# Node stages of a graph-network kernel: loads and stores of one 512-row group each become loads and stores of a 1024-row pair

## The chip, the cores and the metric

The kernel runs on one core of one Trainium2 chip. The metric is device time in microseconds (us) of one execution. All data are float32 and the tables live in HBM.

## The reference, cut to what matters

A table `x` of 50000 nodes by 128 features passes through four residual graph layers over the same 25000 edges (`src`, `dst`, sorted by `dst`):

```
h = relu(layernorm(x)); x = x + relu(segment_sum(h[src] @ W[edge_type], dst) + h @ W_loop + b)   # REL
h = relu(layernorm(x)); x = x + attention(q(h[dst]), k,v(h[src]), softmax over the edges of dst) # ATT
h = relu(layernorm(x)); x = x + sage(relu(layernorm(sage(h))))                                   # SAGE0, SAGE1
h = relu(layernorm(x)); x = x + degree-normalised sum over neighbours and self of h @ W          # GCN
```

## The kernel before, in words

There are five phases: REL, ATT, SAGE0, SAGE1 and GCN. Each has an **edge stage** and then a **node stage**. The edge stage goes through the edges in 49 rounds (`ROUNDS`) of 4 tiles of 128: GpSimd (POOL) gathers source rows, the engines compute messages and sum them over equal destinations, and the sums are scattered to a table in HBM (`sums` or `attsums`). In SAGE0, SAGE1 and GCN the segment sums of all rounds stay in SBUF (`parked`) and are scattered only when the edge stage is over, while the node stage already runs (`scatter_parked`, L854, four indirect DMAs a round). The node stage follows ("chases") these rounds.

The node stage goes through the nodes in 98 groups (`GROUPS`) of 512 rows. A group lies in SBUF as 4 rows a partition (`K = 4`) over 128 partitions; a row of a table between phases has 132 numbers (`W`, 528 B), a row of the input `x` and of `out` has 128. For each group SyncE (SP) loads the rows (`load_x`, L672) and the sums (`load_s`, L699), in SAGE1 also the residual rows (`load_x2`, L708), and stores the result (`store`, L722). The data of one partition in one such DMA are contiguous on both sides, 2112 B (2048 B for `x` and `out`). There are 8 slots each for inputs and results in `ring`, and 8 for sums in `edge_cells`. ScalarE (ACT) normalises, TensorE (PE) turns and multiplies, VectorE (DVE) computes moments, adds and scales; the results of a group are ready 4 to 7 groups after its rows were first touched.

Each engine runs its own list of steps, written by `run_steps`: a list of (step, lag) and a loop over groups; in turn g a step with lag n handles group g - n. Steps wait on semaphores, and an engine takes its instructions strictly in order. For SP the list is `load_x` at lag 0, `load_s` at lag 0, 2 or 3, `load_x2` at lag 5, `store` at lag 6 to 10. A wait in `load_x` is for the slot to be free (`n_turned`, `n_y_used`, `x_added` or `row_ready` of group g - 8). The wait in `load_s` is for the slot and, in the four phases with segment sums, for the scattered rounds that the group needs: their number stands in a small table `due_i` and is read into an SP register for every group (`value_load`, L691 and L697 in the profile, shown as TENSOR_LOAD), and then SP waits for `rounds_landed` (or `kept_landed` in REL). `store` waits for `row_ready` of its group. `out_free` makes the engine that writes a result slot, and `load_x2` on SP, wait until the store 8 groups earlier has landed (`stored`).

In the edge stage of ATT, SP also loads every second group of `rows1` into SBUF ahead of the node stage (`keep_x`), so that the node stage of ATT loads only the other half.

Of the kernel before, what the change touches and what calls it, by code (L numbers as in the profile page):

```python
# [103 lines left out]
def gnn_stack_kernel(nc, x, src, dst, edge_type, w_rel, w_loop, b_loop, w_q, w_k, w_v,  # L104
# [8 lines left out]
    P = 128  # L113
# [27 lines left out]
    LAST_ROWS = N - (GROUPS - 1) * GROUP  # L141
    assert LAST_ROWS % K == 0

# [23 lines left out]
    with ctx:  # L167
# [241 lines left out]
        loaded = [Signal(sem(f"loaded{s}"), 16) for s in range(SLOTS)]  # L409
        loaded_s = [Signal(sem(f"loaded_s{s}"), 16) for s in range(SLOTS)]  # L410
        loaded2 = [Signal(sem(f"loaded2_{s}"), 16) for s in range(SLOTS)]
        stored = [Signal(sem(f"stored{s}"), 16) for s in range(SLOTS)]
# [77 lines left out]

        def loads_before(phase, s):

            return stores_before(phase, s) - (stores_before(1, s) if phase > ATT and s % 2 == 0 else 0)

        def stores_before(phase, s):

            return phase * (GROUPS // SLOTS + (1 if s < GROUPS % SLOTS else 0))
# [16 lines left out]
        def dense(slot):  # L514

            return ring_cells[:, slot * K * W:slot * K * W + K * D].rearrange("p (k d) -> p k d", k=K)

        def kept(phase, g):

            return phase == ATT and g.mod(2) == 0  # L520

        def kept_rows(g):

            return spans[:, bass.ds(g.div(2).scaled(K * W), K * W)].rearrange("p (k c) -> p k c", k=K)

        def x_data(phase, g):

            if kept(phase, g):
                return kept_rows(g)[:, :, 0:D]
            return dense(g.mod(8)) if phase == REL else x_rows(phase, g)[:, :, 0:D]  # L530

        def x_cols(phase, g, c):

            if phase == REL:
                at = g.mod(8) * K * W + K * D + (c - COL_A) * K
                return ring_cells[:, at:at + K]
            return x_rows(phase, g)[:, :, c]

        def x_col(phase, g, k, c):

            if phase == REL:
                at = g.mod(8) * K * W + K * D + (c - COL_A) * K + k
# [3 lines left out]
        def out_data(phase, g):  # L546

            return dense(SLOTS + g.mod(SLOTS)) if phase == GCN else out_rows(phase, g)[:, :, 0:D]

        def x_landed(eng, phase, g):  # L550
            s = g.mod(SLOTS)
            if kept(phase, g):
                eng.wait_ge(s_kept, 16 * ROUNDS)
                return
            eng.wait_ge(loaded[s].sem, loaded[s].after(g.div(SLOTS), loads_before(phase, s)))

        def s_landed(eng, phase, g):
            s = g.mod(SLOTS)
            eng.wait_ge(loaded_s[s].sem, loaded_s[s].after(g.div(SLOTS), stores_before(phase, s)))
# [35 lines left out]
        def _(sp):  # L595
# [24 lines left out]
            for phase in range(5):  # L620

                def keep_x(r):
                    sp.wait_ge(a_h.sem, a_h.after(r))
                    rows = rows1[bass.ds(r.scaled(2 * GROUP), GROUP), :]
                    sp.dma_start(kept_rows(Step(r.i, 2 * r.times, 2 * r.offset)), rows.rearrange("(p k) c -> p k c", k=K))\
                        .then_inc(s_kept, 16)

                if phase == ATT:
                    for s in range(SLOTS):
# [10 lines left out]
                if phase > 0:  # L640
                    for s in range(SLOTS):
                        sp.wait_ge(stored[s].sem, 16 * stores_before(phase, s))

                def span(g):
                    if g.i is None and g.offset == GROUPS - 1:
                        return slice(N - GROUP, N)
                    return bass.ds(g.scaled(GROUP), GROUP)

                def at(g):
                    return bass.ds(g.scaled(1), 1)  # L650
# [1355 lines left out]
```

## Time and profile before

| | |
|---|---|
| Median of 3 runs | 3517.78 us (3517.47 to 3519.11) |
| The profiled execution, its own time | 3518.85 us |
| Its span, first to last instruction | 3517.1 us |
| Instructions | 66658 |
| Moved by DMA | 638.06 MB, 328005 packets |

A span is counted from the first instruction. The five node stages lie at about 527 to 840, 1525 to 1780, 2052 to 2338, 2606 to 2954 and 3225 to 3514 us; the edge stages are between them. Busy times of an engine are sums of its instructions; the DMA share is the mean busy share of the 16 DMA engines; PEclk is the granted TensorE clock as a share of full speed.

### The profile page before, as it was taken

Reading aid. Unit: us, or ns where it says so; the run is one execution under the profiler, and the core shown is the slowest. Engines: PE = TensorE matmul, PEld = TensorE weight load, DVE = VectorE, ACT = ScalarE, POOL = GpSimd, SP = SyncE. Lnnn points to the kernel's source line nnn. Section 1 sums busy time; section 2 is a strip of 40 time slices with the busy share of each in tenths; the row PEclk is TensorE's granted clock in tenths of the full one; section 3 lists DMA queues with packets and bytes.
Section 4 is the critical chain, followed back from the end, with each engine's and each line's share of the span. In section 5 each row is a group of like instructions: output and inputs, shape, how many; then the busy total and the mean of one; then the engine's idle time right before and its main releaser. Section 6 shows DMA issues by size and latency. Waiting matters only on the chain. (4 is left out here: it accounts for less than half of the span.)

```text
span 3517.1 us, 66658 instructions
## 1 busy us (share of the span) xinstructions
PE 2430.4 (69%) x14044; PEld 1912.0 (54%) x14044; DVE 2493.7 (71%) x10828; ACT 1710.1 (49%) x4561; POOL 2471.2 (70%) x2428
## 2 busy tenths in 40 slices
PE   5988878995666665600058887756678885666998
PEld 3444437774555555500058775545567664555777
DVE  6887869995645545469966678864448887556998
ACT  2333327885544444401134467841126664556777
POOL 5777757777888888745567777847778772777774
PEclk9999999998877777755555679975579997557999
DMA  7355539995444444358832269962249996223998
GB/s 268 127 213 218 212 127 292 315 311 168 69 60 62 62 60 62 55 174 268 268 98 52 52 220 317 314 203 53 52 133 353 340 345 198 53 52 110 319 316 287
DMA packets 328005, 638.06 MB, mean 181 GB/s; under 512 B 61062, under 2 KB 89766, under 8 KB 321762
## 3 DMA queue, kind: packets, MB, share of 16 engines
q1 hardware_dynamic: 233176, 501.53, 42.5%
q0 software_dynamic: 90944, 133.85, 17.3%
q10 hardware_dynamic: 3786, 1.65, 0.2%
q14 instruction: 72, 0.59, 0.1%
q8 instruction: 27, 0.44, 0.1%
HBM read 371.35 MB, written 277.04 MB: 184 GB/s over the span
## 5 line engine op out<-in xcount | busy, mean ns | idle before, releaser
L798 POOL DMA_INDIRECT got<-rows,gidx x588 | 602.3, 1024 | 251.7 <-issue 169.9
L854 POOL DMA_INDIRECT sums<-parked,tidx x588 | 603.8, 1027 | 172.2 <-issue 160.8
L1132 ACT ACTIVATE n_h<-ring 128x128 f32<-128x128 f32 x1176 | 484.0, 482 | 153.7 <-issue 115.0
L1411 PE MATMUL bank<-edge_cells,ident 128*128 128x128 f32 x2352 | 460.8, 278 | 0.0
L1268 PE MATMUL bank<-ident,edge_cells 128*128 128x128 f32 x588 | 137.8, 379 | 386.9 <-ACT edge_cells L999 386.2
L1278 PE MATMUL bank<-parked 128*128 128x512 f32 x784 | 367.0, 611 | 52.9 <-DVE parked L1670 46.7
L868 POOL DMA_INDIRECT attsums<-ring,sidx x196 | 312.5, 1595 | 80.6 <-issue 62.8
L1411 PEld LDWEIGHTS bank<-edge_cells,ident 128*128 128x128 f32 x2352 | 363.0, 195 | 0.0
L1562 DVE COPY gidx<-src_i 128x4 int32 (+1 forms) x225 | 43.5, 193 | 409.1 <-DMA got<-rows,gidx 201.9
L1268 PEld LDWEIGHTS bank<-ident,edge_cells 128*128 128x128 f32 x588 | 94.7, 191 | 433.4 <-ACT edge_cells L999 359.5
L1408 PE MATMUL bank<-w_t,n_ht 128*128 128x128 f32 x1568 | 289.0, 299 | 57.3 <-DMA edge_cells<-sums 56.8
L999 ACT ACTIVATE edge_cells<-got 128x128 f32<-128x128 f32 x588 | 242.0, 483 | 137.3 <-DMA got<-rows,gidx 90.0
L1408 PEld LDWEIGHTS bank<-w_t,n_ht 128*128 128x128 f32 x1568 | 225.7, 201 | 109.9 <-DMA edge_cells<-sums 80.6
L1640 DVE TENSOR_TENSOR_SCAN edge_cells<-bank,edge_cells 128x512 f32<-128x512 f32 x196 | 249.8, 1275 | 43.4 <-ACT edge_cells L1024 15.0
L798 POOL DMA_INDIRECT got<-rowsg,gidx x196 | 195.3, 996 | 93.1 <-issue 51.2
L1278 PEld LDWEIGHTS bank<-parked 128*128 128x128 f32 x784 | 144.0, 194 | 212.2 <-issue 166.7
L1348 PE MATMUL bank<-ident,edge_cells 128*128 128x128 f32 x392 | 82.6, 348 | 249.3 <-ACT edge_cells L1072 249.2
L798 POOL DMA_INDIRECT got<-in_x_dram,gidx x196 | 198.0, 1010 | 72.9 <-issue 54.2
L916 POOL DMA_INDIRECT parked<-rows,dst_i x196 | 195.3, 997 | 74.1 <-issue 65.4
L1670 DVE SCALAR_TENSOR_TENSOR parked<-bank,edge_cells 128x512 f32<-128x512 f32 x392 | 242.0, 682 | 5.2 <-issue 5.2
L1384 PE MATMUL bank<-ident,n_h 128*128 128x128 f32 x1176 | 194.7, 290 | 72.5 <-ACT n_h L1132 55.8
L817 POOL DMA_INDIRECT sums<-edge_cells,sidx x148 | 146.1, 987 | 99.3 <-ACT edge_cells L1038 55.0
(191 smaller groups left out, 6444.8 us busy)
## 6 DMA issues: line engine op xcount, KB each, us to landing
edge_cells<-sums SPq DMA_DIRECT2D x392, 264.0 KB
ring<-rows SPq DMA_DIRECT2D x343, 264.0 KB, 4.3
rows<-ring SPq DMA_DIRECT2D x291, 264.0 KB
edge_cells<-attsums SPq DMA_DIRECT2D x98, 264.0 KB
ring<-rowsg SPq DMA_DIRECT2D x98, 264.0 KB
rowsg<-ring SPq DMA_DIRECT2D x97, 264.0 KB
sums<-parked SPq DMA_DIRECT2D x16, 1584.0 KB
attsums<-parked SPq DMA_DIRECT2D x16, 1584.0 KB
```

The costliest lines, as they stand in the source:

```text
L798: pool.indirect_dma_start(out=got[:, b, j, 0:width], out_offset=None, in_=table[:, :], in_offset=bass.IndirectOffsetOnAxis(ap=gidx[:, b, j ...
L854: pool.indirect_dma_start(out=sums[:, :], out_offset=bass.IndirectOffsetOnAxis(ap=tidx[:, r % 4, j:j + 1], axis=0), in_=parked[:, t, :], i ...
L868: pool.indirect_dma_start(out=attsums[:, :], out_offset=bass.IndirectOffsetOnAxis(ap=sidx[:, b, j:j + 1], axis=0), in_=att_out[:, b, j, :] ...
L916: pool.indirect_dma_start(out=parked[:, t, :], out_offset=None, in_=rows1[:, :], in_offset=bass.IndirectOffsetOnAxis(ap=dst_i[:, t:t + 1], ...
L999: last = nc.scalar.activation(e_h[:, b, j, :], got[:, c, j, 0:D], ACT.Relu, bias=got[:, c, j, COL_C:COL_C + 1], scale=got[:, c, j, COL_A:C ...
L1132: last = nc.scalar.activation(n_h[:, b, k, :], x_data(phase, g)[:, k, :], ACT.Relu, bias=x_col(phase, g, k, COL_C), scale=x_col(phase, g, ...
L1268: last = nc.tensor.transpose(bank[0][:, j * P:(j + 1) * P], rows, ident[:, :])
L1278: last = nc.tensor.matmul(bank[1][:, :], lhsT=w_rel_sb[:, rel, :], rhs=e_htm[:, b, rel, :], start=(rel == 0), stop=(rel == NREL - 1))
L1408: last = nc.tensor.matmul(o, lhsT=n_ht[:, b, k * P:(k + 1) * P], rhs=node_w[phase], start=(bias is None), stop=(not summed and k == K - 1))
L1411: last = nc.tensor.matmul(o, lhsT=ident[:, :], rhs=s_rows(phase, g)[:, k, 0:D], start=False, stop=(bias is None or k == K - 1))
L1640: nc.vector.tensor_tensor_scan(run_t[:, b, :], flag_bank[b][:, :], msg_t[:, b, :] if phase == REL else e_ht[:, b, :], 0.0 if fresh else ru ...
L1670: last = nc.vector.scalar_tensor_tensor(out=e_htm[:, b, rel, :], in0=type_bank[b][:, :], scalar=float(rel), in1=e_ht[:, b, :], op0=ALU.is_ ...
```

## The change

Two neighbouring groups form a pair of 1024 rows (`PAIR`, 49 `PAIRS`): a partition now holds 8 consecutive rows of a table, 4224 B (4096 B for `x` and `out`), of which the first group of the pair takes four and the second the other four. SP's node loop runs over pairs, with 4 pair slots (`PAIR_SLOTS`) in the same memory as the 8 group slots. All other engines still work by groups. A wait that asked for group g now asks for the second group of the pair (`second_of`), and `due_i` and the counts for `fetch_dst` are by pairs. SP's list of steps is `load_x`, `store`, `load_x2`, `load_s`, with new lags. `keep_x` keeps every second pair. The last pair has 848 rows and is stored by two DMAs (96 and 10 partitions).

```diff
+    PAIRS = GROUPS // 2
+    PAIR = 2 * GROUP
+    PAIR_SLOTS = 4
...
+        def pair_of(g):
+            return g.div(2)
+        def second_of(h):
+            return Step(h.i, h.times * 2, h.offset * 2 + 1)
...
+        def pair_cells(tensor, first_slot, h, size):
+            at = (first_slot + 2 * h.mod(PAIR_SLOTS)) * K * W
+            return tensor[:, at:at + size]
+        def by_rows(cells):
+            return cells.rearrange("p (k c) -> p k c", k=2 * K)
...
-        def out_free(eng, phase, g):
-            if g.i is None and g.offset < SLOTS:
+        def out_free(eng, phase, h):
+            if h.i is None and h.offset < PAIR_SLOTS:
                 return
-            o = g.back(SLOTS)
-            s = o.mod(SLOTS)
-            eng.wait_ge(stored[s].sem, stored[s].after(o.div(SLOTS), stores_before(phase, s)))
+            o = h.back(PAIR_SLOTS)
+            s = o.mod(PAIR_SLOTS)
+            eng.wait_ge(stored[s].sem, stored[s].after(o.div(PAIR_SLOTS), stores_before(phase, s)))
...
                 def keep_x(r):
+                    if r.mod(2) == 0:
+                        return
+                    h = r.back(1)
                     sp.wait_ge(a_h.sem, a_h.after(r))
-                    rows = rows1[bass.ds(r.scaled(2 * GROUP), GROUP), :]
+                    rows = rows1[bass.ds(h.scaled(PAIR), PAIR), :]
...
-                def load_x(g):
-                    s = g.mod(SLOTS)
+                def load_x(h):
+                    s = h.mod(PAIR_SLOTS)
+                    g = second_of(h)
...
-                    table = node_in[phase]
-                    sp.dma_start(x_data(phase, g) if phase == REL else x_rows(phase, g), table[span(g), :].rearrange("(p k) c -> p k c", k=K))\
+                    rows = by_rows(pair_cells(ring_cells, 0, h, 2 * K * (D if phase == REL else W)))
+                    sp.dma_start(rows, node_in[phase][span(h), :].rearrange("(p k) c -> p k c", k=2 * K))\
                         .then_inc(loaded[s].sem, 16)
...
-                        due = sp.value_load(due_i[0:1, CHASED.index(phase), at(g)], min_val=base, max_val=base + ROUNDS)
+                        due = sp.value_load(due_i[0:1, CHASED.index(phase), at(h)], min_val=base, max_val=base + ROUNDS)
                         sp.wait_ge(rounds_landed.sem, due)
...
-                s_lag = {REL: 2, ATT: 0, SAGE0: 2, SAGE1: 3, GCN: 2}[phase]
-                store_lag = {REL: 9, ATT: 6, SAGE0: 9, SAGE1: 10, GCN: 7}[phase]
-                stages = [(load_x, 0), (load_s, s_lag), (load_x2, 5), (store, store_lag)]
+                store_lag = {REL: 5, ATT: 4, SAGE0: 6, SAGE1: 6, GCN: 4}[phase]
+                stages = [(load_x, 0), (store, store_lag), (load_x2, 3), (load_s, 0 if phase == ATT else 1)]
                 if phase == REL:
-                    stages.append((row_stored, store_lag + 2))
-                run_steps(sp, stages, GROUPS, SLOTS, behind=SLOTS)
+                    stages.append((row_stored, store_lag + 1))
+                run_steps(sp, stages, PAIRS, PAIR_SLOTS, behind=PAIR_SLOTS)
```

The order of SP's instructions in the loop of SAGE0's node stage, before, for one group (ISA and REGISTER_ALU rows are waits and register arithmetic; `edge_cells` holds the sums, `ring` the rows, `rowsg` is the result table):

```order
L672 ISA [waits n_turned]
L672 DMA ring<-rows 128x528
L682 REGISTER_ALU
L697 ISA [waits n_y_used]
L697 TENSOR_LOAD due_i
L697 ISA x2
L699 ISA [waits rounds_landed]
L699 DMA edge_cells<-sums 128x528
L714 REGISTER_ALU
L722 ISA [waits row_ready]
L722 DMA rowsg<-ring 128x528
```

The same place in the changed kernel, for one pair:

```order
L727 ISA [waits n_turned]
L727 DMA ring<-rows 128x1056
L771 REGISTER_ALU
L781 ISA [waits row_ready]
L781 DMA rowsg<-ring 128x1056
L738 REGISTER_ALU
L753 ISA [waits n_y_used]
L753 TENSOR_LOAD due_i
L753 ISA x2
L755 ISA [waits rounds_landed]
L755 DMA edge_cells<-sums 128x1056
```

The number of instructions of a turn is the same, but a turn now serves two groups. The store has moved ahead of the load of the sums, which now stands behind the store's wait.

SP's loop in SAGE1's node stage before, for one group (`stored3` is the semaphore of a store slot, L708 the load of the residual rows):

```order
L697 ISA [waits mid_sd_ready]
L697 TENSOR_LOAD due_i
L697 ISA x2
L699 ISA [waits rounds_landed]
L699 DMA edge_cells<-sums 128x528
L567 ISA
L708 ISA [waits stored3]
L708 DMA ring<-rows 128x528
L714 REGISTER_ALU
L722 ISA [waits row_ready]
L722 DMA rows<-ring 128x528
```

The same place in the changed kernel, for one pair (L765 loads the residual rows):

```order
L727 DMA ring<-rowsg 128x1056
L771 REGISTER_ALU
L781 ISA [waits row_ready]
L781 DMA rows<-ring 128x1056
L765 ISA [waits stored2]
L765 DMA ring<-rows 128x1056
L740 REGISTER_ALU
L753 ISA [waits mid_sd_ready]
L753 TENSOR_LOAD due_i
L753 ISA x2
L755 DMA edge_cells<-sums 128x1056 [waits rounds_landed]
```

Here the wait for an earlier store to land (`stored2`) comes one turn after that store was issued, and the load of the sums is queued behind it. Before, that store had been issued three turns of one group earlier, and the load of the sums came ahead of this wait.

## Rows read from the trace of the kernel before

**Rows 1.** The page: engines busy over the span, and the DMA share in 40 slices.

```profile
PE 2430.4 (69%) x14044; PEld 1912.0 (54%) x14044; DVE 2493.7 (71%) x10828; ACT 1710.1 (49%) x4561; POOL 2471.2 (70%) x2428
...
DMA  7355539995444444358832269962249996223998
```

**Rows 2.** Stretches inside REL, ATT, SAGE0, SAGE1 (two) and GCN; columns as headed.

```profile
core 0: us, PE busy (x) PEld busy (x) DVE busy (x) ACT busy (x) POOL busy (x), PEclk, DMA share, GB/s
...
616.00:704.00 88.00, 81.15 (x603) 67.30 (x603) 87.27 (x605) 71.70 (x201) 66.17 (x67) 1.00 0.97 315
...
1584.00:1672.00 88.00, 0.00 (x0) 0.00 (x0) 87.25 (x452) 10.11 (x34) 43.32 (x35) 0.50 0.82 269
...
2112.00:2200.00 88.00, 68.43 (x391) 48.86 (x390) 72.22 (x329) 69.31 (x181) 67.91 (x79) 0.92 0.98 317
...
2640.00:2728.00 88.00, 73.57 (x542) 61.35 (x540) 78.80 (x338) 56.52 (x181) 72.28 (x72) 0.98 1.02 354
2728.00:2816.00 88.00, 71.73 (x516) 60.49 (x514) 74.91 (x318) 53.27 (x172) 69.00 (x74) 0.96 1.00 337
...
3256.00:3344.00 88.00, 79.29 (x607) 69.02 (x606) 80.04 (x458) 70.01 (x182) 69.63 (x86) 1.00 0.97 319
```

**Rows 3.** DVE lines run once a group (L1958 four times): ns min/median/max, first to last start.

```profile
L1873 DVE SCALAR_TENSOR_TENSOR ring<-bank,ring x98: 650/660/693, 539.9 to 835.3; 128x512 f32<-128x512 f32 x98
...
L1896 DVE TENSOR_TENSOR n_t<-edge_cells,den x98: 691/695/969, 1528.1 to 1775.1; 128x512 f32<-128x512 f32 x98
...
L1907 DVE TENSOR_TENSOR n_t<-bank,edge_cells x98: 654/692/693, 2054.4 to 2331.9; 128x512 f32<-128x512 f32 x98
...
L1949 DVE TENSOR_TENSOR ring<-n_h,ring x98: 676/686/704, 2627.7 to 2953.2; 128x512 f32<-128x512 f32 x98
...
L1958 DVE SCALAR_TENSOR_TENSOR ring<-bank,ring x392: 338/343/353, 3233.7 to 3514.1; 128x128 f32<-128x128 f32 x196
```

**Rows 4.** Waits of SP from 2020 to 2340 us: us in total, times, longest.

```profile
SPq L722 <- DVE ring L1921: 9.1, 7, 2.1
SPq L699 <- POOLq L840: 8.8, 7, 3.1
```

**Rows 5.** Timeline of SP's DMA issues in SAGE0: start, duration.

```profile
2150.13 0.34 SPq L699 DMA_DIRECT2D edge_cells<-sums  x1
2150.74 0.35 SPq L722 DMA_DIRECT2D rowsg<-ring  x1
2151.28 0.34 SPq L672 DMA_DIRECT2D ring<-rows  x1
2153.36 0.33 SPq L699 DMA_DIRECT2D edge_cells<-sums  x1
```

**Rows 6.** Line 697, SP's register load in SAGE0, SAGE1 and GCN.

```profile
L697 SPq TENSOR_LOAD <-due_i x294: 262/698/1214, 2050.8 to 3501.2; - x147
```

**Rows 7.** Waits of the engines: SAGE0 (first two) and SAGE1, us, times, longest.

```profile
ACT n_h L1132 <- DMA ring<-rows: 37.5, 49, 2.1
DVE n_t L1907 <- DMA edge_cells<-sums: 26.0, 34, 3.7
...
PE bank L1408 <- DMA edge_cells<-sums: 51.8, 67, 2.0
```

**Rows 8.** Line 854, POOL's scatters beside SAGE0, SAGE1 and GCN: first to last start.

```profile
L854 POOL DMA_INDIRECT sums<-parked,tidx x196: 966/974/1499, 2042.0 to 2306.5; - x196
...
L854 POOL DMA_INDIRECT sums<-parked,tidx x196: 966/985/2026, 2599.9 to 2888.7; - x196
...
L854 POOL DMA_INDIRECT sums<-parked,tidx x196: 964/972/1025, 3219.3 to 3475.7; - x196
```

**Rows 9.** Two early stretches: tables are zeroed from rows of 12672 B a partition.

```profile
50.00:60.00 10.00, 9.75 (x37) 4.81 (x37) 8.34 (x24) 2.91 (x7) 1.45 (x2) 1.00 0.79 325
60.00:70.00 10.00, 9.75 (x37) 4.80 (x36) 8.88 (x25) 3.39 (x8) 3.95 (x4) 1.00 0.76 311
```

**Rows 10.** The page's DMA issues: the last number is the median us from issue to landing.

```profile
ring<-rows SPq DMA_DIRECT2D x343, 264.0 KB, 4.3
```

More of the change, by code:

```diff
@@ L640, in _, with span, at @@
                 if phase > 0:
-                    for s in range(SLOTS):
+                    for s in range(PAIR_SLOTS):
                         sp.wait_ge(stored[s].sem, 16 * stores_before(phase, s))
[L644 to L650, printed above, removed]
-                def load_x(g):
-                    s = g.mod(SLOTS)
-                    if kept(phase, g):
+                def span(h):
+                    if is_last(h):
+                        return slice(N - PAIR, N)
+                    return bass.ds(h.scaled(PAIR), PAIR)
+                def at(h):
+                    return bass.ds(h.scaled(1), 1)
+                def load_x(h):
+                    s = h.mod(PAIR_SLOTS)
+                    g = second_of(h)
+                    if kept(phase, h):
                         return
@@ L661, in load_x @@
                         sp.wait_ge(x_added.sem, x_added.before(g, SLOTS))
-                    elif phase == SAGE0:
-                        sp.wait_ge(n_turned.sem, n_turned.before(g, SLOTS, first(MATMUL, phase)))
-                    elif phase == SAGE1:
+                    elif phase in (SAGE0, SAGE1):
                         sp.wait_ge(n_turned.sem, n_turned.before(g, SLOTS, first(MATMUL, phase)))
@@ L700, in load_s, with load_x2 @@
                         .then_inc(loaded_s[s].sem, 16)
[L702 removed]
+                def load_x2(h):
                     if phase != SAGE1:
                         return
[L705 to L722 removed]
@@ L725, in row_stored, with store @@
-                def row_stored(g):
-                    s = g.mod(SLOTS)
-                    sp.wait_ge(stored[s].sem, stored[s].after(g.div(SLOTS), stores_before(phase, s)))
+                    s = h.mod(PAIR_SLOTS)
+                    out_free(sp, phase, h)
+                    sp.dma_start(by_rows(pair_cells(ring_cells, SLOTS, h, 2 * K * W)),
+                                 rows2[span(h), :].rearrange("(p k) c -> p k c", k=2 * K)).then_inc(loaded2[s].sem, 16)
+                def store(h):
+                    s = h.mod(PAIR_SLOTS)
+                    sp.wait_ge(row_ready.sem, row_ready.after(second_of(h), phase * GROUPS))
+                    table = node_out[phase]
+                    rows = by_rows(pair_cells(ring_cells, SLOTS, h, 2 * K * (D if phase == GCN else W)))
+                    if is_last(h):
+                        for low, high in ((P - LAST_PARTS, P - LAST_PARTS + LAST_EVEN), (P - LAST_PARTS + LAST_EVEN, P)):
+                            sp.dma_start(table[N - (P - low) * 2 * K:N - (P - high) * 2 * K, :]
+                                         .rearrange("(p k) c -> p k c", k=2 * K), rows[low:high, :, :])\
+                                .then_inc(stored[s].sem, 16)
+                        return
+                    sp.dma_start(table[span(h), :].rearrange("(p k) c -> p k c", k=2 * K), rows)\
+                        .then_inc(stored[s].sem, 16)
@@ L728, in row_stored @@
+                def row_stored(h):
+                    s = h.mod(PAIR_SLOTS)
+                    more = 1 if is_last(h) else 0
+                    sp.wait_ge(stored[s].sem, stored[s].after(h.div(PAIR_SLOTS), stores_before(phase, s) + more))
                     sp.sem_inc(rows_stored.sem, 1)
-                s_lag = {REL: 2, ATT: 0, SAGE0: 2, SAGE1: 3, GCN: 2}[phase]
-                store_lag = {REL: 9, ATT: 6, SAGE0: 9, SAGE1: 10, GCN: 7}[phase]
-                stages = [(load_x, 0), (load_s, s_lag), (load_x2, 5), (store, store_lag)]
+                store_lag = {REL: 5, ATT: 4, SAGE0: 6, SAGE1: 6, GCN: 4}[phase]
@@ L777, in _ @@
                 if phase > 0:
-                    for s in range(SLOTS):
+                    for s in range(PAIR_SLOTS):
                         pool.wait_ge(stored[s].sem, 16 * stores_before(phase, s))
```

121 lines of the change are left out of this document (66 added, 55 removed).

## The prediction

> **What bounds the kernel now.** I read the page first [rows 1]. No engine is above 71% over the span, so no single one is the bound, and the DMA row swings between 2 and 9 tenths: the edge stages leave the DMA engines mostly idle, the node stages fill them. The change touches almost nothing but the node stages, so each of the five was read alone, in stretches of 88 us [rows 2], with the pace of a DVE instruction that runs once a group [rows 3]. Pace is last start minus first start over 97:
>
> - REL: 295.4 / 97 = 3.05 us a group. DVE is busy 87.27 of 88 us, so it needs 3.02 us a group. DVE is the bound.
> - ATT: 247.0 / 97 = 2.55 us. DVE is busy 87.25 of 88 us. DVE is the bound; DMA is at 0.82.
> - SAGE0: 277.5 / 97 = 2.86 us. DVE is busy 72.22 of 88, 2.35 us a group; ACT 2.25. DMA is at 0.98.
> - SAGE1: 325.5 / 97 = 3.36 us. DVE 76.9 of 88 (mean of its two rows), 2.93 us a group. DMA is at 1.01.
> - GCN: 280.4 / 97.75 (four instructions a group) = 2.87 us. DVE 80.04 of 88, 2.61 us; PE 79.29 of 88, 2.59 us. DMA is at 0.97.
>
> So REL and ATT can gain nothing from transfers, and the other three have 0.51, 0.43 and 0.26 us a group that DVE doesn't need. What takes that time? The engines do wait for loads: in SAGE0 ACT 37.5 us for rows and DVE 26.0 us for sums, in SAGE1 PE 51.8 us for sums [rows 7]. Two things can make loads late, and both show. First, the DMA engines are full [rows 2]. Second, SP, which issues the loads, has hardly any wait in 320 us round SAGE0: 9.1 and 8.8 us [rows 4]. Its slots are free and its stores are ready when it comes to them. A queue that is ahead of its consumers would wait for slots; this one never does. Its turn is three DMA issues (0.34 + 0.35 + 0.34 = 1.03 us) and, between the load of rows and the next load of sums, a gap of 1.74 us [rows 5], mostly the register load, 262 ns at best and 698 at the median [rows 6]. With the small instructions between them this fills the 2.86 us. **SP's own instruction stream is the pace of SAGE0, SAGE1 and GCN**, close beside the DMA engines; SAGE1 has one issue more and is 0.50 us slower.
>
> **The change, part by part.**
>
> *SP.* A turn has the same instructions but serves two groups: about 2.9 us for 5.7 us of work (SAGE1 3.4 for 6.7). SP stops being a bound, by a factor of two. Gain on that score: all that DVE leaves free, until something else binds.
>
> *DMA engines, price of a row.* Before there is no plain load or store of 4224 B, so it is bounded. ATT's stretch has no other traffic: 269 GB/s at share 0.82 is 20.5 GB/s an engine while busy, 103 ns for 2112 B [rows 2]. Zeroing with 12672 B rows moves 311 to 325 GB/s at 0.76 to 0.79, 25.6 GB/s an engine, 495 ns a row [rows 9]. Ends: no cheaper a byte (206 ns for 4224 B), or as cheap as 12672 B (165 ns). A line through both rows gives 103 + 2112 x 0.0371 = 181 ns; I take that, 12% off, since 4224 is nearer to 2112. Some five sixths of the traffic in these stages is SP's, the rest POOL's scatters, which don't change. DMA time a group: SAGE0 0.98 x 2.86 = 2.80 us, less 10% = 2.52; SAGE1 3.39, less 10% = 3.05; GCN 2.78, less 10% = 2.50.
>
> *The scatters that the node stages chase.* 196 indirect DMAs serve 98 groups, two a group. Their pace is 264.5 / 97.5 = 2.71 us a group in SAGE0, 2.96 in SAGE1 and 2.63 in GCN, the last almost POOL's own pace [rows 8]. A pair needs the same round as its two groups did (1024 nodes against about 1024 nodes a round), so no wait is added. But a node stage can't end before its scatters. In SAGE0 they end at 2306.5 and the last DVE row starts at 2331.9 in rows 3; in GCN at 3475.7 against 3514.1. A tail of about 12 to 15 us must stay (one pair's load, then the lags).
>
> *Sum of the stages.* The largest need rules. SAGE0: scatters 2.66 against 2.86, 0.20 x 98 = 20 us; held by the scatters' tail I take 18. SAGE1: DMA 3.05 and its unevenness, 3.12; 0.24 x 98 = 23, I take 22. GCN: scatters 2.63 to DVE 2.61 with small gaps, 2.67; 0.20 x 98 = 20, I take 18. REL: 0.03 x 98 = 3 at most, I take 0. ATT: 0.
>
> *Start and end of each stage.* The first load is twice as large and the first store waits for two groups. 270 KB at about 320 GB/s is 0.85 us, once in and once out, less where the other engines are still busy; the last pair takes two DMAs. About +1.2 us x 5 = +6.
>
> *Costed at nothing.* The loads of rows in REL and GCN are issued later against their use. In GCN `load_x` of pair h+1 waits for the row of group 2h-5 (lag 4), so it goes out when DVE is some 2.5 groups before that pair; it was 3.5. That is 6.5 us; a landing takes 4.3 us at the median [rows 10] and 0.85 more for twice the bytes. Cover stands, with 1.4 us to spare; without it each us costs 49 us a stage. The store now stands ahead of the sums and can hold them back: they still go out 3.5 groups (9 us) before use in GCN and ATT, and land after some 5 to 6. In SAGE1 `load_x2` waits for a store issued one turn (6.2 us) before, which should have landed. `keep_x`: 24 DMAs for 49, hidden in the edge stage. POOL's `fetch_dst` in REL: the same rounds behind the same nodes. Instructions of PE, ACT and DVE: unchanged.
>
> Sum: -18 - 22 - 18 + 6 = -52 us. Against the profiled execution's own 3518.85 us that is 3466.9; the median of the runs is 1.1 us lower, and I give 3466.
>
> **The rivals.**
>
> *The bytes bind, not the rows.* If 4224 B cost the DMA engines 206 ns, DMA time stays 2.80, 3.39 and 2.78 us a group, and only the share below 1 is left: 0.06 x 98 = 6 us in SAGE0, 0 in SAGE1, 9 in GCN, less 6 for the ends: about 3509. For it: the share is 0.97 and above in four node stages. Against it: the 25.6 GB/s of the long rows, and that SP doesn't wait.
>
> *A ceiling on the memory side.* SAGE1 already moves 354 GB/s in one stretch, the others 315 to 319 [rows 2]. If about 355 is the most that this core gets, whatever the rows, SAGE1 gains little: its mean is 345, so 3% at best, and 22 shrinks to 8; the other two stay at 18 (they'd move 340): 3480. For it: no stretch of any kind shows more than 354. Against it: zeroing reached its 325 with the engines only 0.79 busy. The Trainium skill ("DMA: Bandwidth & Descriptors", Specifications) puts HBM at about 358 GB/s per core, which speaks for this rival; the same page's larger figures speak against it, and this trace shows no stretch that decides.
>
> *Slower: the pair loads come too late.* The place is `load_x` in REL and GCN and the sums in SAGE1, where the lead shrank or a landing wait came in ahead. It decides when a pair needs longer than its lead of about 2.5 groups: 7.6 us in REL, 6.5 in GCN. If store, sums and rows of a turn queue behind each other, 3 x 1.7 + 3.5 = 8.6 us, so REL would lose 1.0 x 49 = 49 us and GCN, at 2.1 us a pair against a gain of 0.4, about 83. Were half of the pairs hit in both: +66, SAGE0 and SAGE1 -40, ends +6: 3551. Against it: rows are issued at the head of a turn in REL and GCN, when the earlier ones have drained.
>
> *The DMAs don't get longer rows* (a lowering that cuts them at 4 rows): SP's relief stays, the rest is as with the bytes: 3509.
>
> **How the numbers follow.** Forecast 0.54. Bytes bind 0.13 and no longer rows 0.03, both at 3509, 9 us faster, with the ends of the stages as their largest doubt: half of it within 0.2%. Memory ceiling 0.16. Late pairs 0.14. 0.2% is 7 us, about what a measurement of this kernel can tell from no change. Faster: 0.54 + 0.16 + 0.08 = 0.78; same 0.08; slower 0.14. The likeliest case alone: if all three reach their floors (DVE 2.35 with the scatters' tail, -25; 2.93, -42; 2.61, -22; ends at 0) 3430; with half of each gain and ends of +10 3500. The range for 8 in 10 takes in the ceiling and the byte case: 3434 to 3514.
>
> **What would show it.** Right: TENSOR_LOADs halve; SP waits for slots or rows in SAGE0, SAGE1 and GCN; their paces 2.66, 3.12 and 2.67; packets under 8 KB fall by some 70000 or more; REL and ATT keep 3.05 and 2.55; DMA share of SAGE0 falls below 0.98. Wrong: DMA share at 1.0 with the GB/s of before (bytes), SAGE1 stuck at 3.3 and 355 GB/s (ceiling), or DVE in REL or GCN waiting on DMA for rows (late pairs). A larger drop than 85 us would mean the edge stages or REL moved as well, which nothing here explains.

## The result, and the profile after

The changed kernel is slower: 3543.85 us median (3542.24 to 3550.32, 4 runs) against 3518.26 for the kernel before (3517.47 to 3519.11, 4 runs), ratio 1.0074 with a 95% interval of 1.0061 to 1.0086. The forecast was 3466, in a range of 3434 to 3514. The profiled execution took 3542.24 us, its span 3540.5, 23.4 us more than the span of before.

The page of the changed kernel: the rate in 40 slices of the span, and the packets.

```profile
GB/s 266 127 218 219 216 132 282 306 304 151 67 60 60 64 60 64 60 122 266 272 143 52 52 163 320 288 271 52 52 78 377 380 366 176 52 52 129 318 290 279
DMA packets 215273, 637.97 MB, mean 180 GB/s; under 512 B 48578, under 2 KB 77282, under 8 KB 209036
```

The same bytes, in 215273 packets instead of 328005: the rows are longer, as meant. The totals tell no more, so the stages are read again: first the once-a-group DVE lines (they answer to [rows 3], in the order REL, ATT, SAGE0, SAGE1, GCN), then stretches of the stages to lay beside [rows 2]; SAGE1 and GCN start later now, so SAGE1's first stretch is left out and GCN's lies 44 us further on.

```profile
L1933 DVE SCALAR_TENSOR_TENSOR ring<-bank,ring x98: 652/660/692, 538.6 to 833.9; 128x512 f32<-128x512 f32 x98
...
L1956 DVE TENSOR_TENSOR n_t<-edge_cells,den x98: 691/694/1616, 1556.7 to 1803.4; 128x512 f32<-128x512 f32 x98
...
L1967 DVE TENSOR_TENSOR n_t<-bank,edge_cells x98: 650/691/693, 2085.1 to 2364.8; 128x512 f32<-128x512 f32 x98
...
L2008 DVE TENSOR_TENSOR ring<-n_h,ring x98: 673/680/704, 2663.1 to 2962.2; 128x512 f32<-128x512 f32 x98
...
L2017 DVE SCALAR_TENSOR_TENSOR ring<-bank,ring x392: 339/343/352, 3243.5 to 3536.7; 128x128 f32<-128x128 f32 x196
```

```profile
616.00:704.00 88.00, 81.12 (x605) 67.26 (x603) 87.27 (x604) 72.02 (x202) 57.40 (x59) 1.00 0.92 303
1584.00:1672.00 88.00, 0.00 (x0) 0.00 (x0) 87.33 (x457) 10.39 (x35) 44.23 (x36) 0.50 0.75 268
2112.00:2200.00 88.00, 69.61 (x407) 49.38 (x405) 72.77 (x337) 71.66 (x186) 66.38 (x79) 0.94 0.95 319
...
2728.00:2816.00 88.00, 81.53 (x619) 68.73 (x618) 87.96 (x380) 66.70 (x206) 69.00 (x70) 1.00 1.00 382
3300.00:3388.00 88.00, 79.47 (x604) 68.48 (x602) 79.19 (x452) 69.75 (x182) 61.40 (x76) 1.00 0.96 312
```

From these rows the 23.4 us can be laid out. REL and ATT keep their length (295.3 and 246.7 us). SAGE0 is 2 us longer (279.7 for 277.5), SAGE1 26 shorter (299.1 for 325.5), GCN 13 longer (293.2 for 280.4). The largest piece is where the prediction has no term: from REL's last DVE row to ATT's first there are 722.8 us for 692.8, **30 us more**, in an edge stage that the change hardly touches. The rest, the other stretches between and around the stages together, is 5 us.

In REL's stretch above DVE is as busy as before, but POOL runs 59 instructions for 67. Its line there is the fetch of destination rows (`fetch_dst`, L916 before, L976 after), which gathers, round by round, rows that REL's node stage has just stored. Of before, and then of the changed kernel, with the first gather of ATT's edge stage:

```profile
L916 POOL DMA_INDIRECT parked<-rows,dst_i x196: 991/997/1047, 590.8 to 854.2; - x196
```

```profile
L976 POOL DMA_INDIRECT parked<-rows,dst_i x196: 992/997/1047, 591.2 to 882.4; - x196
its engine sat idle before it (us, times) until:
  issue: 96.3, 176
  DMA parked<-rows,dst_i: 5.8, 19
...
886.57 1.02 POOL L858 DMA_INDIRECT got<-rows,gidx  x1 [0.18 <-issue]
```

The same 196 indirect DMAs of 1.0 us now end 28 us later. POOL issues the first gather of ATT's edge stage right behind the last of them, at 886.57 us for 858.69 before, so that stage starts 28 us later too. The timeline of POOL at one moment of REL shows how, before and after (start, duration, idle before):

```profile
704.52 1.00 POOL L916 DMA_INDIRECT parked<-rows,dst_i  x1 [0.30 <-issue]
705.82 0.99 POOL L916 DMA_INDIRECT parked<-rows,dst_i  x1 [0.30 <-issue]
707.12 0.99 POOL L916 DMA_INDIRECT parked<-rows,dst_i  x1 [0.30 <-issue]
```

```profile
703.47 1.00 POOL L976 DMA_INDIRECT parked<-rows,dst_i  x1 [0.30 <-issue]
705.87 1.00 POOL L976 DMA_INDIRECT parked<-rows,dst_i  x1 [1.40 <-issue]
...
709.77 1.00 POOL L976 DMA_INDIRECT parked<-rows,dst_i  x1 [0.30 <-issue]
712.15 1.00 POOL L976 DMA_INDIRECT parked<-rows,dst_i  x1 [1.38 <-issue]
```

Before, a round of four takes 4 x 1.30 = 5.20 us without a gap at this moment. After, every fourth start is 1.1 us late here; over the whole fetch it is 28 us in 49 rounds, 0.6 us a round. The profile puts the gap down to "issue" and names no releaser. What stands there in the code is `dst_landed(r - 1)`: POOL issues round r, then waits until round r - 1 has landed. Before, that wait was nearly always met in time (e5 below takes it away there and gains 2 us in the fetch). The scatters in the node stages have the same form (`round_landed(r - 1)`), and they are slower too: in GCN, 283.9 us for 256.4.

```profile
L914 POOL DMA_INDIRECT sums<-parked,tidx x196: 967/974/1028, 3229.5 to 3513.4; - x196
```

So the theory for the experiments: with the transfers of pairs in place POOL's indirect DMAs land later, and POOL, which waits for each round one round later, has less slack than that. And for SAGE1: its gain comes from relieving SP, not from cheaper rows.

### The profile page after: what moved, and what is told of

Same layout as the page of the kernel before. It is cut to its first block and busy times, and to the rows that moved or that the text cites. A ratio compares the mean times of both kernels' runs of the same rounds, so it can differ in the third digit from the quotient of the medians.

```text
span 3540.5 us, 63369 instructions
## 1 busy us (share of the span) xinstructions
PE 2430.0 (69%) x14044; PEld 1918.2 (54%) x14044; DVE 2487.0 (70%) x10828; ACT 1713.6 (48%) x4561; POOL 2474.9 (70%) x2428
## 2 busy tenths in 40 slices
DMA packets 215273, 637.97 MB, mean 180 GB/s; under 512 B 48578, under 2 KB 77282, under 8 KB 209036
## 5 line engine op out<-in xcount | busy, mean ns | idle before, releaser
L1059 ACT ACTIVATE edge_cells<-got 128x128 f32<-128x128 f32 x588 | 242.0, 483 | 141.0 <-DMA got<-rows,gidx 93.8
L976 POOL DMA_INDIRECT parked<-rows,dst_i x196 | 195.6, 998 | 102.4 <-issue 96.3
L1130 ACT ACTIVATE edge_cells<-got 128x128 f32<-128x128 f32 x196 | 94.8, 484 | 262.1 <-DMA got<-rows,gidx 262.1
```

The source lines that it names most:

```text
L1059: last = nc.scalar.activation(e_h[:, b, j, :], got[:, c, j, 0:D], ACT.Relu, bias=got[:, c, j, COL_C:COL_C + 1], scale=got[:, c, j, COL_A:C ...
```

## The experiments

All times below are medians beside runs of the kernel before on the same chip, and the ratios are to those runs. The medians of the kernel before lay between 3518.3 and 3522.4 us, so a difference between two medians of different experiments is uncertain by some 4 us; the ratios are the safer comparison. Stage times are first to last start of the once-a-group DVE line, from one profile each. Two profiles with the same code in a stage differ there: the changed kernel and e1 have 293.2 and 289.3 us in GCN, with its scatters at 283.9 and 278.7, and e3 and e7 have 269.8 and 263.1 us in SAGE0. Smaller differences than these say nothing.

**e1_fetch: the fetch may run two rounds ahead.** The changed kernel, with

```diff
-        fetched = [... for b in range(2)]
+        fetched = [... for b in range(4)]
...
                         fetch_dst(r)
-                        if r > 0:
-                            dst_landed(r - 1)
+                        if r > 1:
+                            dst_landed(r - 2)
+                    dst_landed(ROUNDS - 2)
                     dst_landed(ROUNDS - 1)
```

> The changed kernel, with one thing different: in REL POOL's fetch_dst waits for a round of gathers only after two more rounds have been issued (four semaphores in place of two), where it waited after one. Theory A (POOL's round loop is paced by the landing of the round before, which the pair loads make later): the gathers' pace returns from 291.2 us for 195 steps to about 263, as before the change, the attention edge stage starts some 28 us earlier, and the time falls from 3543.9 to about 3516. Theory B (the gathers get less of the DMA engines beside rows of 4224 B, whatever POOL waits for): the pace stays near 6.0 us a round and the time within 5 us of 3543.9.

Measured: 3515.0 us, ratio 0.9983 (0.9973 to 0.9992), 29 below the changed kernel's median, 32 by the ratios. The fetch of this kernel:

```profile
L976 POOL DMA_INDIRECT parked<-rows,dst_i x196: 993/1000/1050, 597.5 to 860.2; - x196
```

262.7 us, POOL's own pace, with all pair DMAs in place. ATT's first row comes at 1534.4 instead of 1556.7, though this run's REL began 4 us later. The missing term is this wait.

**e2_scatter: the scatters may run half a round further ahead.** The changed kernel, with four semaphores for the scatters and the wait for round r - 2 in the middle of round r:

```diff
                     for j in range(TPR):
+                        if j == 2 and r > 1:
+                            round_landed(r - 2)
+                            gate(pool)
...
                     for r in range(ROUNDS):
                         scatter_parked(r)
-                        if r > 0:
-                            round_landed(r - 1)
+                    round_landed(ROUNDS - 2)
```

> The changed kernel, with one thing different: in SAGE0, SAGE1 and GCN POOL waits for a round of scatters half a round later (after two tiles of the round after next; four semaphores). Theory A: the scatters' pace beside GCN goes from 2.91 us a group back to about 2.63 and beside SAGE0 from 2.82 to about 2.65, and since these two node stages wait for the rounds, GCN becomes 15 to 25 us and SAGE0 10 to 18 us shorter: about 3510. Theory B (the scatters get less of the DMA engines): both paces and the time stay, 3540 to 3546. A third reading, that the node stages are held by their own late pair loads: the scatters speed up and the stages don't, 3540.

Measured: 3519.39 us, ratio 0.9989 (0.998 to 0.9999). The scatters take 260.6, 287.5 and 252.3 us (changed kernel 275.4, 293.8, 283.9), and the node stages 265.4, 294.0 and 282.7 (279.7, 299.1, 293.2): 14, 5 and 10.5 us less. The median is 24 us below the changed kernel's, 30 by the ratios.

**e3_both: both edits together.**

> The changed kernel with both of the edits to POOL's waits. Theory A: the gains add, 28 + 33 us: about 3483, some 35 us below the kernel before the change. Theory B: no more than 5 us below 3543.9.

Measured: 3488.65 us (3484.69 to 3489.0), ratio 0.990 (0.9883 to 0.9916): 55 us below the changed kernel, about the sum of the two (29 + 24; by the ratios 61 for 32 + 30). With POOL's waits out of the way, SAGE1 is read again, in the same two stretches as in [rows 2]:

```profile
2640.00:2728.00 88.00, 81.54 (x618) 68.67 (x618) 86.61 (x378) 64.27 (x204) 72.12 (x75) 1.00 1.02 393
2728.00:2816.00 88.00, 80.23 (x609) 67.76 (x609) 88.00 (x379) 65.46 (x207) 72.28 (x74) 1.00 1.00 385
```

DVE has no idle time left in the second (88.00 of 88), and 393 GB/s are moved where before 354 was the most of any such stretch. The loss, then, is two waits on POOL. What did the pairs themselves do?

**e4_short_rows: the changed kernel with rows of 2112 B.** A pair is still one DMA of 528 KB, but its two groups lie four slots apart in SBUF, so a partition is two pieces. POOL's waits are those of the change.

```diff
+        def slot_of(g):
+            return g.mod(2) * PAIR_SLOTS + pair_of(g).mod(PAIR_SLOTS)
...
-            at = (first_slot + 2 * h.mod(PAIR_SLOTS)) * K * W
-            return tensor[:, at:at + size]
+            low = first_slot * K * W
+            cells = tensor[:, low:low + 2 * PAIR_SLOTS * K * W].rearrange("p (a s c) -> p a s c", a=2, s=PAIR_SLOTS)
+            return cells[:, :, h.mod(PAIR_SLOTS), 0:size // 2]
```

> The changed kernel, with the two groups of a pair four slots apart in SBUF: still one DMA for a pair, issued at the same moments, but of rows of 2112 B (256 of them) in place of 128 of 4224 B. It tells the length of the rows from the bunching of the DMAs. If POOL's landings are later because each of its packets waits behind a longer row, the gathers in REL go back to about 263 us and the scatters beside GCN to 2.65 us a group: ATT starts 28 us earlier; SAGE1, which gained 26 us, loses most of that if the gain came from cheaper rows. Time about 3530. If the bunching of three pair DMAs does it, the gathers stay at about 291 us, GCN's scatters at 2.9, and the time is at or above 3544.

Measured: 3534.44 us, ratio 1.0038 (1.0024 to 1.0051). The fetch takes 288.2 us (291.2 with long rows), SAGE1 297.9 (299.1), GCN 284.7 (293.2). So the long row does not make the landings late in REL, and it isn't what SAGE1 gained by: rows as short as before keep the gain.

GCN is another matter. Its scatters, with POOL's waits as tight as in the change, come most of the way back with the short rows alone, to 262.8 us from 283.9 (278.7 in e1, which has the changed kernel's code there); before they took 256.4:

```profile
L918 POOL DMA_INDIRECT sums<-parked,tidx x196: 967/974/1026, 3227.8 to 3490.6; - x196
```

The expectation had 2.65 us a group for the case that a landing waits behind longer rows; measured are 262.8 / 97.5 = 2.70, so in GCN that case holds for most of the delay. This rests on one profile of each kernel; that the whole time came out 9 us below the changed kernel's, with the two intervals apart, agrees with it. In SAGE0 the scatters fell by 5 us (270.3), within what two profiles differ by.

**e5_before_both: the kernel before, with both waits relaxed.** The edits of e1 and e2, on the kernel before.

> The kernel before, with both of POOL's waits relaxed (a round's landing is waited for one round later in the fetch of REL, and half a round later in the scatters). Theory: a relaxed wait pays only where landings are late, and in the kernel before they come just in time: the fetch stays at 263 us, the scatters of SAGE0, SAGE1 and GCN go from 264.5, 288.8 and 256.4 to at best 260, 286 and 252, the node stages SAGE0, SAGE1 and GCN stay within 3 us of 277.5, 325.5 and 280.4; total 3512 to 3520. Rival, that the two waits were a cost of the kernel before as well and the pairs have no part in it: its node stages fall to those of e3_both (270, 293, 283) and the total to about 3490.

Measured: 3517.59 us, ratio 0.999 (0.9981 to 1.0); fetch 261.6, node stages 276.9, 329.8 and 280.9. In the kernel before the two waits cost next to nothing, at most 7 us by the interval; the pairs made them count.

**e6_before_no_register_loads: the kernel before, with SP's register loads left out.** The number of rounds that a group needs is worked out from the loop counter (g // 2 + 2, and exact constants in the unrolled part) instead of being read from `due_i`, in REL as well as in the three stages named in the expectation. In the loop this asks for one round more than most groups need, so the edit can hide a part of the gain in SAGE0 and GCN but can't make one up. The edit in those three stages:

```diff
-                        due = sp.value_load(due_i[0:1, CHASED.index(phase), at(g)], min_val=base, max_val=base + ROUNDS)
+                        due = base + DUE[g.offset] if g.i is None else g.div(2).scaled(1, base + 2)
                         sp.wait_ge(rounds_landed.sem, due)
```

> The kernel before, in which SP works the scatter rounds that it waits for out of its loop counter and constants instead of loading them into a register: 98 register loads fewer in each of the three stages that chase the scatters (0.7 us each at the median), all else alike, so the DMAs are the same in number and size. Theory that SP's own instruction stream set the pace of SAGE0 and SAGE1: SAGE1 goes from 325.5 to 300 us or less, SAGE0 from 277.5 to about 268 (its scatters' pace), GCN from 280.4 to about 276 (2.81 us a group, the loop between ACT and DVE); total about 3480. Rival, that the DMA engines set the pace through the price of a 2112 B row: the paces stay, and the total is within 5 us of before.

Measured: 3490.35 us (3487.94 to 3494.93), ratio 0.9913 (0.9896 to 0.9929). SAGE1 takes 300.8 us for 325.5, with the DMAs of before in number, size and row. SP's timeline in SAGE1, of before and then of e6: between the load of rows (L672, L673) and the load of sums (L699, L700) SP was held for 1.5 us, now for 0.3.

```profile
2738.50 0.34 SPq L672 DMA_DIRECT2D ring<-rowsg  x1
2740.35 0.33 SPq L699 DMA_DIRECT2D edge_cells<-sums  x1
```

```profile
2737.90 0.33 SPq L673 DMA_DIRECT2D ring<-rowsg  x1
2738.54 0.33 SPq L700 DMA_DIRECT2D edge_cells<-sums  x1
```

From 2640 to 2900 us SP had waited 4.4 us for results to store and 0.4 us for scatters. In e6 it waits for them many times as long (us, times, longest), as a queue does that is ahead of the others:

```profile
SPq L723 <- DVE ring L1950: 39.5, 54, 1.7
SPq L700 <- POOLq L841: 19.8, 19, 2.9
```

And SAGE1's second stretch in e6: 380 GB/s with rows of 2112 B, where the same rows moved 337 before, and at share 1.04.

```profile
2728.00:2816.00 88.00, 79.01 (x594) 66.18 (x594) 85.97 (x370) 62.25 (x199) 68.78 (x69) 1.00 1.04 380
```

A share of 1.00 had been read as full engines. It wasn't the limit. SAGE0 gave only 2 us (275.0), with its scatters now at 269.9, and GCN 2 (278.1); both are taken up in e9.

**e7_gcn_rows_by_group: e3, and in GCN the rows of a pair by two DMAs**, each as soon as its own slot is free:

```diff
+                    if phase == GCN:
+                        halves = node_in[phase][span(h), :].rearrange("(p a k) c -> p a k c", a=2, k=K)
+                        for a, landed in ((0, loaded), (1, loaded2)):
+                            one = Step(h.i, h.times * 2, h.offset * 2 + a)
+                            sp.wait_ge(row_ready.sem, row_ready.before(one, SLOTS, phase * GROUPS))
+                            sp.dma_start(x_rows(phase, one), halves[:, a, :, :]).then_inc(landed[s].sem, 16)
+                        return
```

> e3_both, and in GCN each pair's rows are loaded by two DMAs, one per group, each as soon as its own slot is free, so the first goes out a group earlier; sums and stores stay pairs. Theory that in e3_both GCN is slower than before (283.5 against 280.4) because the rows of a pair come late to DVE: GCN falls to 276 to 279 us, near 98 x 2.81 us, and DVE's wait for rows falls from 24.7 us in 315 to 12 or less; total 3482 to 3485. Rival, that the loop between ACT and DVE alone sets GCN: 283 us stay, and the total is that of e3_both.

Measured: 3477.59 us (3475.51 to 3480.25), ratio 0.9876 (0.9859 to 0.9892), the fastest here. GCN takes 272.4 us, more gain than either theory had. DVE's wait for rows in GCN, in the changed kernel (its stage), in e3 and in e7 (stretches 3200 to 3484 and 3200 to 3470):

```profile
DVE in_stats L1856 <- DMA ring<-rows: 24.7, 26, 2.8
```

```profile
DVE in_stats L1861 <- DMA ring<-rows: 14.8, 28, 2.4
```

```profile
DVE in_stats L1868 <- DMA ring<-rows: 2.5, 3, 2.0
```

Before it was 11.6 us. (The text on record puts e3's wait at 24.7 us; that is the changed kernel's, e3's is 14.8.) So the late pair load was real, in GCN alone and at some 11 us (e3's median less e7's, and their GCN stages), where the slower rival had 83.

**e8_both_short_rows: e3 with rows of 2112 B**, by e4's edit.

> e3_both with rows of 2112 B: a pair is still one DMA, but its two groups lie four slots apart in SBUF, so each partition is two rows. Theory that in e3_both the cheaper row of 4224 B does little, since DVE and the scatters bind: SAGE0 270 to 273, SAGE1 292.6 to 298, GCN 283 to 285, total 3490 to 3500. Rival, that the cheaper row carried the gain of SAGE1 and SAGE0: SAGE1 310 or more, SAGE0 278, total 3515.

Measured: 3492.9 us, ratio 0.992 (0.9903 to 0.9936); SAGE0 262.2, SAGE1 295.3, GCN 284.5. Where nothing else is in the way, the longer row is worth about 4 us of 3489, 7 by the ratios, and the intervals of e3 and e8 overlap. (SAGE0's 262.2 for 269.8 is no gain: e7 has e3's code there and 263.1.)

**e9_groups_no_loads_both_waits: no pairs at all.** e6's and e5's edits together, on the kernel before.

> The kernel before with its group DMAs, no register loads on SP (as e6_before_no_register_loads) and both of POOL's waits relaxed (as e5_before_both). Theory that the pairs do nothing for the time but relieve SP: SAGE0 falls from e6's 275.1 to 263 to 268 us (its scatters run at POOL's own pace), SAGE1 stays at 297 to 301, GCN at 273 to 278, total 3477 to 3485, level with the best version with pairs (3477.59). Rival, that longer rows and fewer DMAs carry a part of their own: SAGE1 stays at 300 or above and SAGE0 at 270 or above, total 3488 or more.

Measured: 3479.91 us (3475.26 to 3481.21), ratio 0.9888 (0.9871 to 0.9904), level with e7. SAGE0 266.9, SAGE1 299.5, GCN 277.7. One DMA per group and 2112 B rows do as well as the best version with pairs. Once SP is relieved, POOL's waits seem to cost something: some 9 us between e6 and e9 by their ratios, whose intervals overlap by a little.

**e10_pairs_as_two_dmas: the changed kernel, each pair load and store as two group DMAs, one behind the other.** This asks whether the size of one DMA or the bunching in time makes POOL's landings late.

```diff
+                    for a in (0, 1):
+                        one = Step(h.i, h.times * 2, h.offset * 2 + a)
+                        sp.dma_start(s_rows(phase, one), node_sum[phase][span(h), :]
+                                     .rearrange("(p a k) c -> p a k c", a=2, k=K)[:, a, :, :]).then_inc(loaded_s[s].sem, 16)
```

> The changed kernel with SP's steps and waits by pairs as they are, but every load and store of a pair issued as two group DMAs of 2112 B rows, one right behind the other: the size of a DMA is that of before, the moments are those of the change. POOL's waits as in the change. Theory that it is the bunching in time that makes POOL's landings late, whatever the size of a DMA: the fetch in REL takes 280 to 292 us, the scatters of GCN 265 to 284, SAGE1 297 to 303, total 3530 to 3550. Rival, that it is the size of one DMA: the fetch returns to 263 to 266 us, the scatters of GCN to 256 to 258, total 3505 or less.

Measured: 3496.66 us (3493.77 to 3503.92), ratio 0.9936 (0.9919 to 0.9952). My theory missed. The fetch takes 269.2 us and GCN's scatters 260.9, close to before, with POOL's waits as tight as in the change and SP still working by pairs:

```profile
L981 POOL DMA_INDIRECT parked<-rows,dst_i x196: 991/997/1047, 597.0 to 866.2; - x196
...
L919 POOL DMA_INDIRECT sums<-parked,tidx x196: 964/973/1025, 3204.8 to 3465.7; - x196
```

The time is 22 us below the kernel before: with SP's turns by pairs, so half of the register loads, but no DMA enlarged, the pairs are a gain even with POOL's waits left alone. But e10 changes more than the size of a DMA. Its rows are short, as in e4, and for GCN e4 has the same result without splitting anything (262.8). And the moments had moved too. SP's timeline in REL, of the changed kernel and of e10 (x2 is two issues): three issues within 2.3 us, and six spread over 4.6.

```profile
639.78 0.34 SPq L727 DMA_DIRECT2D ring<-in_x_dram  x1
640.38 0.36 SPq L781 DMA_DIRECT2D rows<-ring  x1
641.69 0.34 SPq L755 DMA_DIRECT2D edge_cells<-sums  x1
```

```profile
641.44 0.85 SPq L728 DMA_DIRECT2D ring<-in_x_dram  x2
642.49 0.89 SPq L787 DMA_DIRECT2D rows<-ring  x2
645.10 0.89 SPq L758 DMA_DIRECT2D edge_cells<-sums  x2
```

**e11_pairs_spread: the changed kernel, with the sums of a pair sent out half a pair later**, in REL and GCN. One DMA of 528 KB each, as in the change.

```diff
+                    half = Step(h.i, h.times * 2, h.offset * 2 + 4)
+                    if phase == REL and (h.i is not None or h.offset >= 3):
+                        sp.wait_ge(n_y_used.sem, n_y_used.before(half, SLOTS, first(MATMUL, phase)))
+                    if phase == GCN and (h.i is not None or h.offset >= 3):
+                        sp.wait_ge(row_ready.sem, row_ready.before(half, SLOTS, phase * GROUPS))
```

> The changed kernel with the load of a pair's sums in REL and GCN held back by half a pair (it waits for the event of one group more), so that it goes out about 3 us after the load of rows and the store of its turn instead of 1 to 2 us; sizes, counts and POOL's waits are those of the change. Theory that landings are late because three pair DMAs go out together: the fetch falls from 291 to 265 to 275 us, the scatters of GCN from 284 to 260 to 270, total 3500 to 3515. Rival, that one DMA of 528 KB is enough to hold a landing up wherever it stands: the fetch stays at 283 to 292, the scatters of GCN at 275 to 285, total 3535 to 3550.

Measured: 3545.07 us (3542.54 to 3549.68), ratio 1.0072 (1.0055 to 1.0089), the changed kernel's time. The sums now go out 3.7 us after the store (645.69, then 649.39):

```profile
645.10 0.33 SPq L727 DMA_DIRECT2D ring<-in_x_dram  x1
645.69 0.35 SPq L787 DMA_DIRECT2D rows<-ring  x1
649.39 0.35 SPq L761 DMA_DIRECT2D edge_cells<-sums  x1
```

and the fetch takes 291.3 us all the same, GCN's scatters 278.7:

```profile
L982 POOL DMA_INDIRECT parked<-rows,dst_i x196: 991/997/1047, 595.8 to 887.1; - x196
```

For the fetch in REL, short rows don't help (e4, 288.2), holding back the sums doesn't (291.3), and splitting each DMA, which also spreads the issues, does (269.2). So the size of one DMA, 528 KB instead of 264, is the likeliest cause there. It isn't shown alone: the load and the store still went out 0.6 us apart in e11, and no run spreads these two at full size. For the scatters in GCN the length of the row carries most (e4, 262.8; e10, with short rows as well, 260.9; e11, with long ones, 278.7). How an indirect DMA comes to wait behind such transfers is not visible in any view here and stays open.

## Why the prediction was wrong

By its own steps, the sum expected -52 us and the spans differ by +23.4. The step that failed is what the pairs do to POOL's loops: the fetch was costed at nothing and the scatters' pace was carried over.

- **"POOL's `fetch_dst` in REL: the same rounds behind the same nodes", costed at nothing: +30 us.** This is the largest error. The rounds and nodes are the same, but each round waits for the landing of the one before, and with the pairs' transfers beside it that landing came later (fetch 291.2 us for 263.4). I had not read POOL's timeline in REL: four issues of 1.30 us are 5.20 us, and no row of mine said how much of that the landing left free. e1 shows the term by taking it away (-29, by the ratios -32).
- **The scatters' pace, taken as unchanged ("so no wait is added").** I had set 2.66 and 2.63 us a group; they ran at 275.4 / 97.5 = 2.82 and 283.9 / 97.5 = 2.91. (The 2.66 of SAGE0 has no row behind it: the same prediction reads 2.71 from [rows 8], and with that the term shrinks from 20 to 15 us.) That is most of why SAGE0 lost 2 us instead of gaining 18, and GCN 13 instead of gaining 18. e2 gave back 14 and 10.5.
- **GCN's floor, DVE busy 2.61 us a group.** Even with free scatters (e3, 283.5) GCN isn't faster than before. A part was the late load of rows: the step "Cover stands, with 1.4 us to spare" fails, and e7 gives back 11 us. The step had a landing at 4.3 + 0.85 = 5.15 us against a lead of 6.5; for all loads from `rows` the page of the changed kernel has 6.8 us at the median:

```profile
ring<-rows SPq DMA_DIRECT2D x172, 528.0 KB, 6.8
```

The rest is no engine's busy time. ACT's and DVE's timeline of before, one group of GCN:

```profile
3300.32 1.65 ACT L1132 ACTIVATE n_h<-ring 128x128 f32<-128x128 f32 x4 [0.49 <-issue]
3301.23 0.86 DVE L1796 BATCH_NORM_STATS2 in_stats<-ring 128x6 f32<-128x128 f32 x4
3301.88 0.28 ACT L1120 ACTIVATE in_sd<-in_mv,eps_col 128x4 f32<-128x4 f32 x1
...
3302.19 0.18 DVE L1837 RECIPROCAL in_rstd<-in_sd 128x4 f32<-128x4 f32 x1
...
3302.91 0.14 DVE L1852 SCALAR_TENSOR_TENSOR ring<-in_mv,ring 128x4 f32<-128x4 f32 x1
...
3303.13 1.65 ACT L1132 ACTIVATE n_h<-ring 128x128 f32<-128x128 f32 x4 [0.49 <-issue]
```

The period is 3303.13 - 3300.32 = 2.81 us though no engine is full: ACT normalises, takes the root for the next group, DVE makes scale and shift of it in small operations, and ACT starts the next normalisation just behind. e7's 272.4 / 97.75 = 2.79 is close to that period. That this loop sets it is argued from the timeline; no run here shortens it.
- **SAGE1: -26.4 against -22. Right in size by luck: the price of rows had little to do with it.** The term said "DMA 3.05": cheaper rows. But e6 gets 300.8 us with the old rows, e4 297.9 with short rows in pairs. The sentence ahead of the sum, that SP's own instruction stream is the pace, is what holds for SAGE1. ("Mostly the register load" was read loosely there: the load's median is 0.70 of a gap of 1.74 us; e6, which leaves out the load and the small instructions with it, shortens such a gap by 1.2.) For SAGE0 and GCN it holds only together with the scatters: e6 alone gives 2 us each, e9 11 and 3, against profiles that differ by 4 to 7.
- **The price of 4224 B, 181 ns.** ATT has no other traffic: share 0.75 at 268 GB/s against 0.82 at 269 in [rows 2], 8% less, about 189 ns by the same working as on record. Within its ends of 165 and 206. It just wasn't what bound: e8 puts the long rows at 4 to 7 us, and e4 shows that beside GCN's scatters they did harm.
- **Starts and ends: +5 for +6.** The 5 us lie between the stages' rows and needn't all be starts and ends. REL and ATT's node stages: 0, right. `keep_x`: nothing seen.
- **The rivals.** The memory ceiling of about 355 GB/s falls: this kernel has slices of 377 and 380 GB/s, e3 a stretch of 393. The trace of before could have told: it was read in stretches of 88 and 10 us, and in slices of 2.2 us SAGE1 reached 401 there. The Trainium skill ("DMA: Bandwidth & Descriptors", Specifications) puts HBM at about 358 GB/s per core, half of a stack's rate for each of two cores. This kernel runs on one core and goes beyond it with reads and writes together, and the measurement decides. The bytes that bind fall with e6. The rows did get longer (215273 packets for 328005), so the rival of a lowering that cuts them falls too. The slower rival named the right sign with the wrong place: it had pair loads late for DVE in REL and GCN. REL showed none of it (DVE 87.27 of 88), GCN some 11 us. What was late was another queue's landing.

## What to carry to other kernels

Before you enlarge the transfers of one queue, list every loop on another queue that waits for its own landing, and read its slack from the timeline: issue time of a round less the landing. Here 5.2 us a round had too little left, and about 29 and 24 us were lost in loops that the change doesn't touch; letting the fetch run a round further ahead, and the scatters half a round, gave them back. A DMA share of 1.00 doesn't prove that the engines are the bound: take a few instructions from the issuing queue first and see whether the GB/s rise. Leaving out a register load (31 us of 3522 by e6) brought as much as the pairs did with POOL's waits relaxed (e3, ratio 0.990 for e6's 0.9913), and is a far smaller edit.

## What was not expected of the hardware

- Beside DMAs of 528 KB another queue's loop of indirect DMAs ran slower, where beside two of 264 KB, issued back to back, it hardly did: fetch 291.2 us against 269.2, with 263.4 before. For this loop of gathers the length of the rows (288.2) and a later load of the sums (291.3) made no difference. For the loop of scatters in GCN the length of the rows did: 283.9 and 278.7 us beside rows of 4224 B, 262.8 beside 2112 B at the same size of a DMA, 256.4 before.
- With rows of 2112 B the busy share stood at 1.00 at 337 GB/s and at 1.04 at 380 GB/s, in the same stretch of before and of e6. The share had reached 1 before the rate was at its top; why is not shown.
- In SAGE1 SP's step with the register load held it for 1.5 us between two DMA issues, where the load itself shows 0.7 at the median [rows 6]; without the load 0.3 remained. In the changed kernel, which issues half as many DMAs from this queue, the median of the same load is 337 ns; what makes it shorter is not shown:

```profile
L753 SPq TENSOR_LOAD <-due_i x147: 262/337/1562, 2080.4 to 3523.2; - x147
```
